# A three-part forward pass in f32: weight loads, small products and row statistics in another order

## The reference

```python
tok = wte[input_ids]
Q = layer_norm(tok, gamma, beta) @ W_proj.T          # 8 heads of 64
V = tok @ W_val.T
Q_erase = Q_store / norm(Q_store)                    # Q_store: Q of the tokens that the mask keeps
erase = einsum('bhip,bhiq->hpq', Q_erase, V_old) / denom
v_update = einsum('bhip,bhiq->hpq', Q_store, V_store) / denom
traces = 0.99 * (value_traces - erase) + 0.1 * v_update
h = (shifted Q @ traces) @ W_out.T
x1 = layernorm(h); q, k, v = split(x1 @ W_qkv + b_qkv)   # attention with 49 group weights
h = h + attention(q, k, v);  h = h + mixture_of_64_experts(layernorm(h))
```

## Time and profile before

| what | us |
|---|---|
| median of 3 runs | 500.75 (499.6 to 500.93) |
| the profiled execution's own time | 499.41 |
| its span (first to last instruction) | 497.6 |
| PE busy in the span | 450.2 (90%) |
| DVE, ACT, POOL busy | 305.7, 215.2, 145.4 |
| granted TensorE clock, mean | 0.964 |

### The profile page before, as it was taken

How to read it: one execution, slowest core, us unless ns; L and a number is a source line. 1 busy time by engine, 2 the same in 40 slices (tenths; PEclk the granted TensorE clock), 3 DMA queues, 4 the chain that set the end, 5 groups by cost and what they waited for, 6 DMA issues and landing times.

```text
span 497.6 us, 8397 instructions
## 1 busy us (share of the span) xinstructions
PE 450.2 (90%) x3098; PEld 364.8 (73%) x3098; DVE 305.7 (61%) x829; ACT 215.2 (43%) x398; POOL 145.4 (29%) x235
## 2 busy tenths in 40 slices
PE   5599999799669999999999899999649599999996
PEld 2387756797558888888888788899525387777785
DVE  4689853585844756767775857668522154455475
ACT  2387641399524336644224848163661212112220
POOL 4887400373100262210003930034211221223110
PEclk9999998899879999999999999999978979999999
DMA  8111000003000000400000000027057999997104
GB/s 295 45 42 34 1 2 0 0 2 109 16 0 0 1 1 9 183 1 0 1 0 2 2 0 2 0 88 295 0 200 302 386 345 405 387 375 275 31 27 126
DMA packets 14200, 49.65 MB, mean 100 GB/s; under 512 B 3472, under 2 KB 8496, under 8 KB 9936
## 3 DMA queue, kind: packets, MB, share of 16 engines
q1 hardware_dynamic: 6992, 41.64, 22.0%
q10 hardware_dynamic: 4256, 4.10, 2.4%
q0 software_dynamic: 2912, 3.37, 2.4%
HBM read 45.94 MB, written 3.15 MB: 99 GB/s over the span
## 4 chain that ended last, share of the span: by engine, by line
PE 75%; DVE 7%; ACT 6%; DMA 5%; POOL 4%; issue 3%; ACTq 0%; POOLq 0%; DVEq 0%
PE ps L1053 10%; PE ps L864 9%; PE ps L910 6%; PE ps L1005 4%; PE ps L1030 3%; PE ps L846 2%; PE ps L1041 2%; PE ps L677 2%; DMA ys<-ys_dram 2%; PE ps L890 2%; ACT ec L1271 2%; PE ps L819 2%; PE ps L582 2%; PE ps L893 1%; PE ps L891 1%
## 5 line engine op out<-in xcount | busy, mean ns | idle before, releaser
L1053 PE MATMUL ps<-ys,ct 128*128 128x192 f32 x256 | 52.0, 357 | 5.1 <-DMA ys<-ys_dram 5.1
L1793 DVE SCALAR_TENSOR_TENSOR res<-ps,riC,res 128x192 f32<-128x192 f32 x128 | 46.7, 413 | 12.1 <-PE ps L1053 9.6
L1053 PEld LDWEIGHTS ps<-ys,ct 128*128 128x128 f32 x256 | 41.5, 197 | 15.0 <-issue 8.5
L864 PE MATMUL ps<-pr,et 128*128 128x192 f32 x256 | 46.4, 332 | 2.1 <-DVE et L1641 1.6
L864 PEld LDWEIGHTS ps<-pr,et 128*128 128x128 f32 x256 | 41.1, 189 | 5.2 <-ACT et L1249 3.1
L485 POOL TENSOR_SCALAR ve<-mv 128x1 f32<-128x1 f32 x32 | 12.9, 403 | 103.5 <-DVE mv L1656 61.4
L1354 ACT ACTIVATE hs<-ps 128x384 f32<-128x384 f32 x16 | 7.9, 491 | 79.9 <-PE ps L1005 79.9
L570 POOL DMA_DIRECT2D ys<-ys_dram x32 | 19.7, 619 | 73.9 <-DMA ys_dram<-ysb 68.1
L1238 ACT ACTIVATE scs<-ps,pr 128x1024 f32<-128x1024 f32 x16 | 17.9, 1117 | 41.1 <-PE ps L823 41.1
L1784 DVE COPY ysb<-ps 128x192 f32<-128x192 f32 x16 | 5.7, 358 | 46.8 <-PE ps L1030 46.8
L1242 ACT ACTIVATE zz<-zz,nmx 128x1024 f32<-128x1024 f32 x16 | 18.4, 1150 | 26.4 <-DVE nmx L1635 26.3
(11 more groups left out here) (323 smaller groups left out, 1197.6 us busy)
## 6 DMA issues: line engine op xcount, KB each, us to landing
w1r<-in_p_w SPq DMA_DIRECT2D x16, 1152.0 KB, 11.8
w2r<-in_p_w SPq DMA_DIRECT2D x16, 1152.0 KB, 9.2
ys_dram<-ysb ACTq DMA_DIRECT2D x16, 96.0 KB, 7.7
ys<-ys_dram POOLq DMA_DIRECT2D x32, 48.0 KB, 6.9
phT<-in_p_phi SPq DMA_DIRECT2D x1, 1024.0 KB, 4.8
wT<-in_p_qkv ACTq DMA_DIRECT2D x1, 774.0 KB
out<-res SPq DMA_DIRECT2D x4, 192.0 KB, 3.2
out<-res ACTq DMA_DIRECT2D x4, 192.0 KB, 3.9
```

Of the source, the lines that this page charges most:

```text
L864: last = mm(d[:, 0:D], et[:, k, :], pr[:, b * KT + k, 0:D], start=(k == 0), stop=(k == KT - 1))
L1053: mm(bank(5 + q % 3)[:, 0:D], ct[:, u % 2, k, :], ys[:, t % YR, b, :], start=True, stop=True).then_inc(m["yp_filled"], 1)
L1793: v.scalar_tensor_tensor(res[:, i, :], bank(5 + q % 3)[:, 0:D], riC[:, i:i + 1], res[:, i, :], ALU.mult, ALU.add).then_inc(m["yp_taken"], 1)
```

## The change

1. **Loads.** Only `ints`, `wpT`, `cols` and `ident` are loaded at once. The others go to SP, which first waits for the statistics of two tiles (`front_stats` at 2). An activation of one column on ACT stands ahead of its first wait, so that the table is loaded there.
2. **Start.** POOL gathers three tiles instead of four ahead of `front_factors(0, 1)`, and the fourth before `front_factors(1, 3)`. The products for the head pairs (eight calls, 16 instructions) move from PE's start to a place between `mix` and `prepare("kB2")`. `stats(3)` moves from ahead of DVE's loop into it, and each step ends with `stats(s + 3)`.
3. **Bias column.** The query bias is column 257 of the query product, and the two products of one column in each `prepare("v..")` go. In `pr` and in the value weights the bias is the first column instead of the last.
4. **End of the first loop.** `grams` runs through all 16 tiles in the loop, `weigh(1)` stands ahead of `grams(14)`, and `prepare("kA")` behind `grams(15)`.
5. **Between the loops.** `prepare("vA")`, `"vB1"`, `"vB2"` move into steps 0, 1 and 3 of the second loop; the rounding to steps 1, 2 and 4 of ACT and DVE. Before "nB2" PE waits for "kB2" to be taken by DVE, since DVE then also copies the pair products into `wpn`.

```diff
         def _(sp):
             sp.dma_start(ints[:], a["p_ints"]).then_inc(m["in_ids"], 16)
             sp.dma_start(wpT[:], a["p_wp"]).then_inc(m["in_wp"], 16)
+            sp.wait_ge(m["front_stats"], 2)
+            sp.dma_start(wT[:], a["p_qkv"]).then_inc(m["in_attn"], 16)
+            sp.dma_start(wpg[:], a["p_wpg"]).then_inc(m["in_attn"], 16)
+            sp.dma_start(wvT[:], a["p_wv"]).then_inc(m["in_mix"], 16)
+            sp.dma_start(vt[:], a["p_vt"]).then_inc(m["in_mix"], 16)
+            sp.dma_start(woT[:], a["p_wo"]).then_inc(m["in_mix"], 16)
             sp.dma_start(wpn[:], a["p_wpn"]).then_inc(m["in_mix"], 16)
-            sp.dma_start(wvT[:], a["p_wv"]).then_inc(m["in_mix"], 16)
...
-            for g in range(4):
+            for g in range(3):
                 gather(g)
             front_factors(0, 1)
+            gather(3)
+            front_factors(1, 3)
             gather(4)
-            front_factors(1, 3)
...
-                    mm(d[0:n, D + G:W2N], wTq[:, 0, lo:lo + n], bks[:, 0:1], start=True, stop=False)
-                    filled(mm(d[0:n, D + G:W2N], wTq[0:DB, 1, lo:lo + n], bks[0:DB, 1:2], start=False, stop=True))
...
-                if 5 <= s < NT + 4:
+                if s == NT + 3:
+                    weigh(1)
+                if 5 <= s:
                     grams(s - 5)
                 if s == NT + 2:
-                    prepare("kA", 1)
                     weigh(0)
-                if s == NT + 3:
-                    weigh(1)
-                    prepare("kB1", 0)
-            prepare("kB2", at["kA"] + 1)
+            prepare("kA", 1)
...
-            grams(NT - 1)
-            prepare("vA", 0)
...
-            prepare("vB1", at["kB2"] + 1)
+            prepare("kB1", 0)
...
-            prepare("vB2", at["vA"] + 1)
+            pe.wait_ge(m["setup_taken"], at["kA"] + 1)
+            beta_of_pairs()
+            prepare("kB2", at["kA"] + 1)
...
+            pe.wait_ge(m["setup_taken"], at["kB2"] + 1)
...
             for s in range(NT + 5):
                 if s < NT:
                     mixed(s)
+                if s == 0:
+                    prepare("vA", 0)
+                if s == 1:
+                    prepare("vB1", 0)
                 if 3 <= s < NT + 3:
                     x1_T(s - 3)
+                if s == 3:
+                    prepare("vB2", at["vA"] + 1)
...
-            stats(3)
...
-                if s + 4 < NT:
-                    stats(s + 4)
+                if s + 3 < NT:
+                    stats(s + 3)
...
             for s in range(NT + 4):
+                if s in (1, 2, 4):
+                    round_v({1: "vA", 2: "vB1", 4: "vB2"}[s])
```

More of the change, by code:

```diff
@@ L193, in build @@
         fac = sb("fac", [P, NT, HEADS], where=front)
+        wT = sb("wT", [P, 3, 2, PC], where=front)
+        wTq, wTk, wTv = (wT[:, y] for y in range(3))
+        wpg = sb("wpg", [P, 2, D + G], where=front)
         wpn = sb("wpn", [P, HP, PC], where=front)
@@ L201, in build @@
         cc = sb("cc", [P, 2, D], where=front)
+        cols = sb("cols", [P, 9 + NT + D], where=front)
+        gamA, gamB, gamR = (cols[:, c:c + 1] for c in range(3))
+        betA, betB = cols[:, 3:5], cols[0:DB, 5:7]
+        valid, bproj = cols[:, 9:9 + NT], cols[:, 9 + NT:9 + NT + D]
+        XH = sb("XH", [P, 2, NB * SLOTS * Q], F32R, front)
+        XL = sb("XL", [P, 2, NB * SLOTS * Q], F32R, front)
+        x1t = sb("x1t", [P, 3, XC], where=front)
         nAh = sb("nAh", [P, D], F32R, front)
@@ L231, in build @@
         prs = sb("prs", [P, 2, NP], where=biases)
[L232 to L236, removed]
+        KV = XC + W2N
+        sb("beyond", [P, W1N + W2C - NE - HID - D - 2 * NT - 4 * NP - 4 * KV], where=biases)
+        kv = [sb(f"kv{part}", [rows, KV], F32R, biases) for part, rows in (("Ah", P), ("Al", P), ("B1", P), ("B2", DB + 2))]
+        kAh, kAl, kB1, kB2 = (t[:, 0:XC] for t in kv)
+        vAh, vAl, vB1, vB2 = (t[:, XC:KV] for t in kv)
         biases.close()
@@ L360, in pass_tiles @@
             return []
-        SETUP = ["beta", "kA", "kB1", "kB2", "vA", "vB1", "vB2", "nB2", "nB1", "nA"]
-        SETUP_BANK = [7, 7, 3, 7, 6, 7, 6, 7, 4, 5]
+        SETUP = ["beta", "kA", "kB1", "kB2", "nB2", "nB1", "nA", "vA", "vB1", "vB2"]
+        SETUP_BANK = [7, 7, 6, 7, 6, 4, 5, 5, 6, 5]
         at = {n: k for k, n in enumerate(SETUP)}
@@ L623, in _ @@
             mm(d[DB:DB + 2, :], betA, wpT[:, 0, :], start=True, stop=False)
[L624 to L628, removed]
+            last = mm(d[DB:DB + 2, :], betB, wpT[0:DB, 1, :], start=False, stop=True)
             filled(last)
@@ L800, in beside_scores @@
                         i = b * KT + k
-                        last = mm(d, gw[:, i, :], pr[:, i, 0:D], start=(k == 0), stop=(k == KT - 1))
+                        last = mm(d, gw[:, i, :], pr[:, i, 1:1 + D], start=(k == 0), stop=(k == KT - 1))
                     last.then_inc(m["u_filled"], 1)
@@ L1128, in round_up @@
                 last.then_inc(m["setup_hi"], 1)
             def round_k(name):
-                round_up(name, (SCALE, SCALE, SCALE), kAh, kB1, kB2, XC)
+                Ah, _, B1, B2 = (t[:, 0:XC + 1] for t in kv)
+                round_up(name, (SCALE, SCALE, SCALE), Ah, B1, B2, XC + 1)
             def round_v(name):
-                round_up(name, (1.0, 1.0, 1.0), vAh, vB1, vB2, W2N)
+                Ah, _, B1, B2 = (t[:, XC + 1:KV] for t in kv)
+                round_up(name, (1.0, 1.0, 1.0), Ah, B1, B2, D + G)
@@ L1180, in _ @@
             last.then_inc(m["mm_ready"], 1)
-            round_v("vB2")
-            for name in SETUP[-3:]:
+            round_k("kB2")
+            for name in SETUP[4:7]:
                 round_n(name)
             for s in range(NT + 6):
+                if s in (1, 2, 4):
+                    round_v({1: "vA", 2: "vB1", 4: "vB2"}[s])
                 if 4 <= s < NT + 4:
@@ L1416, in round_off @@
                 if part == "A":
-                    last = remainder(Al[:], d[:, 0:n], scale[0], Ah[:])
+                    last = remainder(Al, d[:, 0:n], scale[0], Ah)
                 elif part == "B1":
@@ L1422, in round_off @@
                     last = v.tensor_scalar(B2[DB:DB + 1, :], d[DB:DB + 1, 0:n], scale[3], None, ALU.mult)
+                if name == "kB2":
+                    last = v.tensor_copy(wpn[:, :, XC:PC], setup_bank(name)[:, 400:400 + 2 * HP].rearrange("p (t c) -> p t c", c=2))
                 last.then_inc(m["setup_taken"], 1)
             def round_k(name):
-                round_off(name, [SCALE] * 4, kAh, kAl, kB1, kB2, XC)
+                round_off(name, [SCALE] * 4, *(t[:, 0:XC + 1] for t in kv), XC + 1)
             def round_v(name):
-                round_off(name, [1.0] * 4, vAh, vAl, vB1, vB2, W2N)
+                round_off(name, [1.0] * 4, *(t[:, XC + 1:KV] for t in kv), D + G)
             def round_n(name):
-                round_off(name, (gamA, gamB[DB:P], gamR[DB:DB + 2], gamR[DB:DB + 1]), nAh, nAl, nB1, nB2, D)
+                round_off(name, (gamA, gamB[DB:P], gamR[DB:DB + 2], gamR[DB:DB + 1]), nAh[:], nAl[:], nB1[:], nB2[:], D)
             def stats(i):
@@ L1529, in _ @@
             v.tensor_tensor(tt[DT:P], traces(1)[DT:P], tt[DT:P], ALU.add).then_inc(m["tt_ready"], 1)
-            round_v("vB1")
+            round_k("kB1")
             dve.wait_ge(m["mix_done"], 2)
             v.tensor_copy(mm_[:, 1:HP:2, :], bank(3).rearrange("p (t c) -> p t c", t=2)[:, :, 0:D]).then_inc(m["mm_ready"], 1)
-            round_v("vB2")
-            for name in SETUP[-3:]:
+            round_k("kB2")
+            for name in SETUP[4:7]:
                 round_n(name)
```

101 lines of the change are left out of this document (42 added, 59 removed).

## The result

| | before | after |
|---|---|---|
| median | 500.18 (4 runs, 499.4 to 500.93) | 511.65 (4 runs, 509.01 to 514.03) |
| profiled execution, its span | 499.41, 497.6 | 514.03, 512.2 |
| granted clock, mean | 0.964 | 0.952 |

The change makes the kernel slower: after / before is 1.0228, 95% interval 1.0174 to 1.0283. The forecast was 507.7 in a range of 502.0 to 512.5.

The account below looks back on a forecast made before the run. PE was taken to bound the first loop, where its waits are paid in full, and POOL to pace the second. −1.1 + 7.2 − 1.6 + 2.0 + 0.5 = +7.0 gave 506.4 for the profiled execution, 507.7 as median; range 502.0 to 512.5.

Parts of the forecast that it names:

- First loop: Later statistics make PE wait before cprime of tiles 4, 6, 8 and 10: +7.2 us, the largest term.
- The cycle: First loop: two tiles take 7.4 us instead of 5.70 through DVE, POOL, PE and ACT; three such cycles cost 5.0.
- The first two rivals: First loop: delay paid once, 2.2 us at cprime(4), 502.3, chance 0.10; or no wait at all, 500.0, chance 0.10.
- Start: Up to cprime(0): tile 0 comes earlier without the loads, four gathers stand behind POOL's power; net −1.1 us.
- tile 4 has 2.1 us to spare at the median: Start: the reason given for taking −1.1 us although gather 4 is issued into the loads.
- the bad bound: Start: gather 4, issued into the loads, takes gather 0's 6.3 us; the term becomes +1.3.
- Between the loops: Value products gone −5.56, pair products +2.5, new wait before "nB2" +1.5: net −1.6 us.
- 5.56 for the value products: Between the loops: time freed by moving the three value prepares away, 1.83, 1.83 and 1.90 us.
- Second loop: Value products ahead of the fifth tile's statistics make POOL late, kept to the end: +2.0 us.
- Clock: First loop: PE's new waits can bring the clock down to 1.2 GHz: +0.5 us, bounds 0 and 4.3.
- falls in every cycle: First loop: rival in which the clock falls in every cycle, +4.3 instead of 0.5, 511.5; chance 0.20.
- 1.53 us did: Before the first x1_T: PE's 1.53 us idle was said to bring the clock down, against the skill's rule.

Follow-up runs that it names:

- e4: The changed kernel with the held loads issued only after the statistics of five tiles instead of two: 509.24, ratio 1.0188 to before.
- e1: The changed kernel with stats(3) ahead of DVE's loop again and stats(s + 4) ending each step: 503.55, ratio 1.0071 to before.
- e2: The kernel before with only the statistics moved: stats(3) into DVE's first loop, stats(s + 3) ending each step: 507.02, ratio 1.0134 to before.
- e10: The changed kernel with late statistics kept, but POOL's pairs shifted to front_factors(i + 2, i + 4) ahead of even tiles: 499.54, ratio 0.9995 to before.
- e9: e6 with PE's wait before "nB2" for DVE to take "kB2" kept, though it protects nothing there: 496.5, ratio 0.9907 to before.
- e6: e5 with the head-pair products back at PE's start and no wait before "nB2": 496.25, ratio 0.9907 to before.
- e8: The changed kernel with five unread products of 512 columns put into PE's wait before "nB2": 509.03, ratio 1.0162 to before.
- e3: The changed kernel with all loads issued at once again and the first gathers in their old order: 509.75, ratio 1.0177 to before.
- e5: The changed kernel with the edits of e1 and e4 together: 502.03, ratio 1.0055 to before.
- e11: e7 with POOL's pairs as in e10 and stats(3) directly behind stats(2): 493.12, ratio 0.9846 to before.
- e7: e6 with "vA" in the pause before the first mixed, "vB1" behind the fourth mixed, "vB2" behind the second x1_T: 493.73, ratio 0.9887 to before.
- e12: e5 with five unread products of 512 columns put into PE's pause before "nB2": 499.34, ratio 0.9986 to before.

## Why the prediction was right or wrong

The direction and the main mechanism were right; the value was 4 us low. The range held the median with 0.85 to spare, in part by luck: its upper end was there for the gather and for a clock that falls in the first loop, and what filled it was the gather, a price read at half clock and a clock that fell elsewhere.

- **First loop, +7.2 forecast, +8.0 in the trace, right.** e4 shows it with no half clock in it: 0.67 earlier than before at `cprime(0)`, 7.20 later at `cprime(15)`, 7.9 in all. The cycle was 7.49, not 7.4, so three cost 5.4 instead of 5.0, and `cprime(4)` came 2.4 later instead of 2.2. e1 removes it, e2 brings it alone, e10 cuts the chain at POOL. The first two rivals are out.
- **Start, −1.1 forecast, +1.1 in the trace, wrong.** The step that failed is "tile 4 has 2.1 us to spare at the median". Its gather was issued into the loads and took 5.7 us, near the 6.3 that I had given as the bad bound; the bound, +1.3, was the right value. Even without it (e4) the start gained 0.7 and not 1.1, since PE's beta product began at 5.17 there instead of 4.6, and POOL's power for tiles 1 and 2 at 12.17 instead of 11.7. The Trainium skill (DMA: Bandwidth & Descriptors, section on queues, rings and completion order) has the engines take turns between queues with work. I had drawn from it that one loaded queue delays a gather less than two; 5.7 against 6.3 agrees in sign, but decides nothing here.
- **Between the loops, −1.6 forecast, +1.6 in the trace.** Two parts were right: pair products 2.5 (forecast 2.5), wait 1.62 in the trace and 1.5 by e9 against e6 (forecast 1.5). The third, 5.56 for the value products, was too large: its 1.90 for "vB2" is the distance from 85.51 to 87.41, which begins inside before's own slow stretch (83.0 to 86.25). At full clock, in e2, it is 1.52. At full clock on both sides the stage takes 26.95 (e8) against 27.78 (e2's, before's code): −0.8. This reading explains 0.4 of the 0.7 that is missing; the rest isn't traced. The clock turned the sign: 31.05 − 26.95 = 4.1 in the changed kernel, 1.6 in before, net 2.5. Part of that belongs to this one execution: e1, e3, e4 and e5, with the same code there, take 29.46 to 29.70.
- **Second loop, +2.0 forecast, +1.5 in the trace** and in e5 and e6. The statistics of the fifth tile come 111.08 − 103.21 = 7.87 after the first `mixed` (forecast 8.1). The first `x1_T` comes at 4.76. About 0.3 us of it is regained later. The clock has no part in this: e2 takes 24.12 from the first `mixed` to the last `x1_T` at full clock, and before takes 24.12 with its slow stretch.
- **Clock, +0.5 forecast, mis-sized and incomplete.** In the first loop, where I had put it, it cost 0.1 in the trace (8.0 against e4's 7.9): there the slow matmuls take their time from the next wait, as the forecast said. In e8, the same code up to there, it cost 1.5 (9.3). It also fell between the loops, which I had not priced (the 2.5 above). Behind the second loop the profiled pair differs by 2.3 more; between 160 and 490 us half clock lasts 23.9 us against 17.1 before. The rival "falls in every cycle" (511.5) comes nearest in time and is wrong in its place. My ground for the term falls too: I had read that the pause of 1.53 us brought the clock down, but e2 has that pause and the 0.96 ahead of it and keeps full clock, and before's clock had fallen once already, at 83.0, with no idle row of PE from 60 on. The Trainium skill (TensorE: Matmul & The Clock Gate, section "Why this matters for your kernels") names longer pauses of PE as what to avoid. The forecast's answer to it, "1.53 us did", isn't borne out; but in before at 83.0 and in e11 at 73.75 the clock fell while PE was busy, with no pause ahead of it, so pauses are not all that matters here.
- **The sum.** 1.11 + 7.97 + 1.64 + 1.54 = 12.26 up to the gelu, and 2.3 more in this execution, the slowest of the four. By the medians the change costs 11.5.

What stays open: why the clock falls between the loops. Six executions with the pair products behind `mix` and the pause ahead of "nB2" (the changed kernel, e1, e3, e4, e5, e10) had half clock there for 3.25 to 10.25 us; of two with filler one had 3.25 us and one none; e6, e7 and e9, without pair products there, had none. In the changed kernel (91.0, amid the pair products), e1 (84.8) and e5 (82.2) it fell before the pause began, so the pause isn't what it takes, and the pair products are a suspect. They aren't needed for it either: before had 3.25 us there and e11 had 6.75 at an earlier place, both without them, while e2, with before's code, had none. Each of these is one execution.

## What to carry to other kernels

Before a producer is moved one step later, follow what waits for it through the queues of all engines. Here a factor computed for later tiles stood ahead of `xm` in POOL's queue, so that under 1 us of work on DVE, a step late, stopped PE for 1.5 us in every second tile. Asking in that queue for the nearest tiles' factors only (e10) freed both the loop and the start.

Bulk loads that are delayed can collide with the next gather instead of the first: here 5.7 us for tile 4 instead of 6.3 for tile 0. Hold them until the last gather that the start waits for has landed (e4: `cprime(0)` 1.8 us earlier). Products of two columns belong where PE is idle anyway: on the path they cost 2.5 us here, and in seven of the eight executions that had them there the clock was at half near or behind them, whether by their doing or not.

## What the runs showed that I had not expected

- PE's clock fell without a pause, in before at 83.0 and in e11. In e11 PE is busy for 6.75 of 6.75 us from 73.75 on at 0.50; ahead of it stand `update` products of 128 columns from 69.99, and no idle row from 60 on.
- Added work made the kernel faster: five useless products (e12) took e5 from 502.03 to 499.34.
- The start could be had 3.2 us earlier than before (`cprime(0)` at 17.87 in e10) with the loads where the change puts them: what the first `xm` is queued behind mattered more than when tile 4 lands.
